# A four-layer graph network on one core: three gather passes go by tile of 128 edges, and edges are ranked four tiles at a time

## The chip, the core and the metric

The kernel runs as one program on one core of a Trainium2 chip. TensorE (PE) multiplies matrices into PSUM, VectorE (DVE), ScalarE (ACT) and GpSimd (POOL) work on SBUF and PSUM, SyncE (SP) here only issues and waits for DMAs. The engines run their own instruction lists and wait for each other by semaphores. The metric is the device time in microseconds (us) of one execution.

## The reference

12,500 nodes with 128 features, 212,500 edges (one loop per node among them) sorted by destination, eight edge types. Each layer takes `h = relu(layernorm(x))`, sums over edges, and adds the result to `x`:

```python
def _rel_graph_conv(x, W, W_loop, b, src, dst, etypes, num_nodes):      # layer 0, twice, relu between
    xw = jnp.einsum('nd,rdh->rnh', x, W)
    agg = jax.ops.segment_sum(xw[etypes, src], dst, num_segments=num_nodes)
    return agg + x @ W_loop + b
# layer 1: edge_index = stack([src, dst]), so rows are summed by SOURCE
h = x @ W.T + b
agg = jax.ops.segment_sum(h[col], row, N) / (cnt + 1e-08)
h = h + agg;  out = batchnorm(h) * gamma + beta
# layer 2: attention with 4 heads over the edges of a source (segment max, exp, sum)
# layer 3: mean of the rows that arrive
sums = jax.ops.segment_sum(x[edge_src], edge_dst, N) / max(counts, 1)
```

## The kernel before

Nodes stand as 98 blocks of 128 in SBUF (`X`, `ACC`, node in its partition). Edges in order of destination form `ET` = 1661 tiles of 128. A **step** is one tile together with one block of nodes: where a tile's destinations lie in two blocks, the tile has two steps. There are at most 1758 steps, padded to `NS` = 1760, in `NG` = 220 groups of `K` = 8; four groups (`RING` = 4) are in flight. Tables made in the first stage say for each step which block it belongs to (`BREGA`) and which edge each partition has (`IDXA` the row of the table, `DLOA` the destination less the block's first node); registers are loaded from such tables by `words_of` (line 436).

A sum over edges, as in `plain_pass` (lines 1031 to 1087), works step by step. ACT copies the indices of eight steps (line 1045), POOL issues eight indirect DMAs that gather 128 rows each (`gather`, line 1025), DVE builds eight one-hot matrices in one instruction (`one_hot`, line 970) and PE multiplies one-hot by rows (line 1085), which sums the rows of a node; DVE adds each product to its block in `ACC`, at an address from a register (line 1074). `groups` and `ringed` write the loops, four groups to an iteration, each with its slots and semaphores.

The order of the stages: `tables_and_first` (rows of the first table TAB for eight relations on PE, and beside them the edge tables on DVE, POOL and PE, put between PE's blocks by hand with `upto`), `ranked_pass`, `dense`, `plain_pass` "g1", `square`, `scatter_pass`, `message_pass`, batch norm, `square`, `largest_pass`, `attention_pass`, a short stage, `plain_pass` "g3".

Layer 1 needs sums by source, so `ranked_pass` (lines 1089 to 1198) also finds each edge's place in the order of sources: `RK` in PSUM holds, for each partition and block of sources, how many edges came before. For each step PE adds the strictly upper triangle times the one-hot of the key (`KO`, line 1192), DVE reads `RK` at the edge's own key (line 1149), then PE adds the rest (line 1197), so PE and DVE take turns for each step. Edges that don't belong to the step's block get a key that matches nothing, and a place beyond the end. `scatter_pass` (lines 1200 to 1279) fetches for each edge the row of its destination by a product with the turned one-hot and scatters it to its place in MSG, one indirect DMA a step (line 1275); DVE prepares the source (line 1233), ACT the places (line 1214). `message_pass` reads MSG in order.

## Time and profile before

| | us |
|---|---|
| median of 3 runs (lowest to highest) | 13794.56 (13775.52 to 13798.18) |
| the profiled execution, its own time | 13784.63 |
| its span, first to last instruction | 13782.6 |
| busy: POOL, PE, DVE, ACT | 9051.3 (66%), 8229.3 (60%), 7417.8 (54%), 1688.7 (12%) |
| mean granted TensorE clock | 0.70 |

Busy shares are averages over stages with different limits: what bounds a stage is read from who waits in it. Instructions that work on registers, branch, issue or wait aren't counted as busy. The time that an indirect DMA shows on POOL is that of making its descriptors, not of moving the rows.

### The profile page before, as it was taken

To read this page: it belongs to the slowest core of one execution; us is meant where nothing else is said; L and a number is where in the kernel's file an instruction comes from. 1 tells how busy PE (TensorE), PEld (TensorE's weight loads), DVE (VectorE), ACT (ScalarE), POOL (GpSimd) and SP (SyncE) were. 2 spreads that over 40 slices of the span, in tenths; PEclk is the share of its full clock that TensorE was granted. 3 is DMA by queue.
4 is the path that set the end of the run, shared out by engine and by line. 5 is a ranking of instruction groups with operands and counts; after the bars stand their busy time and mean duration, and the time that the engine had idled before them with its cause. 6 is when DMAs were issued, how large, how long until landed. Compare 5 with 4: busy or idle time off the path is not lost. (4 is left out here: it accounts for less than half of the span.)

```text
span 13782.6 us, 185595 instructions
## 1 busy us (share of the span) xinstructions
PE 8229.3 (60%) x41562; PEld 5943.6 (43%) x41563; DVE 7417.8 (54%) x19952; ACT 1688.7 (12%) x3723; POOL 9051.3 (66%) x9488
## 2 busy tenths in 40 slices
PE   8555555743333345454546969999998993333333
PEld 4444444433333344444445743333336772333333
DVE  4666666533333343332336977777778884333333
ACT  4000000100000011111110021111113552000000
POOL 0777777367777757777773127777775554777776
PEclk9666666865555565656567978888889996555555
DMA  4222212422212211111114833333333433222222
GB/s 175 64 53 53 53 53 53 147 75 53 53 53 53 53 54 49 50 50 50 50 50 130 205 98 106 106 104 106 104 105 112 127 126 78 54 54 54 54 54 66
DMA packets 715974, 1096.30 MB, mean 80 GB/s; under 512 B 181713, under 2 KB 490913, under 8 KB 715892
## 3 DMA queue, kind: packets, MB, share of 16 engines
q0 software_dynamic: 282496, 584.15, 16.4%
q1 hardware_dynamic: 301480, 449.08, 9.8%
...
## 5 line engine op out<-in xcount | busy, mean ns | idle before, releaser
L1027 POOL DMA_INDIRECT G<-HROW,IDS x3520 | 3334.2, 947 | 1451.8 <-issue 1120.3
L1027 POOL DMA_INDIRECT G<-TAB,IDS x3520 | 3327.1, 945 | 1405.8 <-issue 1072.0
L1085 PE MATMUL PSUM<-G,OH 128*128 128x128 f32 (+1 forms) x7040 | 1645.6, 427 | 2894.5 <-DMA G<-HROW,IDS 1506.5
L1085 PEld LDWEIGHTS PSUM<-G,OH 128*128 128x128 f32 x7040 | 1527.7, 329 | 3012.2 <-issue 2816.9
L1074 DVE TENSOR_TENSOR ACC<-ACC,PSUM 128x128 f32 (+1 forms) x3520 | 1017.1, 289 | 2855.2 <-PE PSUM L1085 2409.6
L1275 POOL DMA_INDIRECT MSG<-G,IDS x1760 | 1734.4, 985 | 649.3 <-issue 584.8
L1589 DVE TENSOR_REDUCE SM<-PSUM 128x8 f32<-128x1024 f32 x880 | 1074.4, 1221 | 390.3 <-PE PSUM L1527 379.1
L1193 PE MATMUL PSUM<-G,OH 128*128 128x128 f32 x3520 | 1197.2, 453 | 0.0
L1262 PE MATMUL PSUM<-ACC,SCR 128*128 x3520 | 812.1, 424 | 628.4 <-ACT SCR L1218 628.0
L971 DVE TENSOR_TENSOR OH<-PSUM,DLOA 128x1024 f32<-128x1024 f32 x880 | 1073.1, 1220 | 94.4 <-DVE POSA L1166 55.4
L1262 PEld LDWEIGHTS PSUM<-ACC,SCR 128*128 128x128 f32 x3520 | 754.8, 326 | 699.6 <-issue 699.6
L1192 PE MATMUL PSUM<-SCR,USTB 128*128 128x98 bf16 x1760 | 473.5, 269 | 910.3 <-DMA G<-TAB,IDS 715.3
L992 PE MATMUL PSUM<-G,OH 128*128 128x129 f32 (+1 forms) x7040 | 881.6, 279 | 29.5 <-DVE OH L971 27.5
L992 PEld LDWEIGHTS PSUM<-G,OH 128*128 128x128 f32 x7040 | 840.3, 191 | 106.3 <-issue 88.2
L1193 PEld LDWEIGHTS PSUM<-G,OH 128*128 128x128 f32 x3520 | 881.5, 307 | 0.0
L1716 POOL TENSOR_TENSOR G<-G 128x1024 f32<-128x1024 f32 x220 | 555.0, 2523 | 418.7 <-ACT G L1742 418.7
L1240 DVE COPY G<-PSUM 128x256 f32<-128x256 f32 x880 | 332.7, 420 | 772.7 <-PE PSUM L1262 772.4
L1527 PE MATMUL PSUM<-SCR,WT 128*128 128x512 bf16 x1760 | 722.4, 410 | 0.0
L1526 PE MATMUL PSUM<-SCR,WT 24*128 24x512 bf16 x1760 | 693.4, 394 | 0.0
L1149 DVE CUSTOM_DVE_ANT_0 HT<-PSUM,SCR 128x98 f32<-128x98 f32 x1760 | 456.3, 259 | 421.6 <-PE PSUM L1192 410.3
L1539 PE MATMUL PSUM<-USTB,LINB 128*128 128x512 bf16 x1760 | 661.2, 544 | 0.0
L999 DVE TENSOR_TENSOR ACC<-ACC,PSUM 128x1188 f32 x440 | 611.0, 1389 | 89.5 <-PE PSUM L992 89.3
...
## 6 DMA issues: line engine op xcount, KB each, us to landing
KEEP<-G SPq DMA_DIRECT2D x220, 528.0 KB, 2.8
G<-KEEP SPq DMA_DIRECT2D x220, 528.0 KB, 3.5
...
G<-TAB,IDS POOLq DMA_INDIRECT x3520, 2.5
G<-HROW,IDS POOLq DMA_INDIRECT x3520, 2.5
...
```

What stands on the lines that cost most here:

```text
L971: return q.tensor_tensor(OH[:, r % 2], bcast(iota.unsqueeze(1), P, K, P), bcast(dlo[:, bass.ds(g * K, K)].unsqueeze(2), P, K, P), op)
L992: return q.matmul(window(n)[:, bass.ds(off, w)], hot, rows, start=False, stop=False, skip_group_check=True)
L1027: q.indirect_dma_start(G[:, r, k, 0:row], None, table, bass.IndirectOffsetOnAxis(ap=IDS[:, r, k:k + 1], axis=0)).then_inc(s_got[r], 16)
L1074: q.tensor_tensor(a, a, sums(r, k), ALU.add).then_inc(s_add, 1)
L1085: m = q.matmul(sums(r, k), OH[:, r % 2, k, :], G[:, r, k, 0:w], start=True, stop=True)
L1193: m = q.matmul(slot(kk)[:, 0:w], OH[:, r % 2, kk, :], G[:, r, kk, 0:w], start=True, stop=True)
L1262: m = q.matmul(slot(h * 4 + k)[:, 0:D], SCR[:, h, k * P:(k + 1) * P], acc_of(regs[h * 4 + k], D), start=True, stop=True)
L1275: q.indirect_dma_start(MSG, bass.IndirectOffsetOnAxis(ap=IDS[:, r, k:k + 1], axis=0), G[:, r, k, :], None, bounds_check=E - 1, oob_is_err= ...
L1526: q.matmul(bank, SEL[:, k, :], ROWS[r % 2], start=True, stop=False)
L1527: m = q.matmul(bank.rearrange("p (h e) -> p h e", h=HEADS), NEGI, bcast(TURN[r % 2][:, k, :].unsqueeze(1), P, HEADS, P), start=False, stop ...
L1539: q.matmul(PS[6], LINB[:], bcast(USTB[:].unsqueeze(1), P, 4, P), start=True, stop=True)
L1589: q.tensor_reduce(reduced(n), PSUM[:, (n % 2) * 1024:(n % 2 + 1) * 1024].rearrange("p (h e) -> p h e", e=P), AX.X, ALU.max).then_inc(s_red, 1)
```

## The change

`ranked_pass`, `plain_pass` "g1" and "g3" gather by tile of 128 edges: `NTG` = 208 groups of eight tiles, each into one of the four slots of the ring. Steps stay for the products: `SLOTS` gives for each step where in `G` its tile lies (an address in a register), and for each group of steps how many tile groups must have landed; SP counts landings into one semaphore (`tile_landings`). `LASTA` gives for each tile group the step group after which its slot may be written again; ACT loads it and waits before it copies the indices. `IDXA` and the places `POSA` are now by tile, `DLOA` by step.

Ranks are made per tile, four at once: PE makes the counts inside four tiles (`within`, products of 392, 294, 196 and 98 columns), DVE copies `RK`, adds, multiplies by the one-hot of the keys and sums (`places`, twice a group), and PE adds the four to `RK` (`counted`). What belongs to the step's block is decided in `scatter_pass`, where DVE fetches place and source of each step by its tile (sixteen one-column instructions) and makes the target from them.

The tables stage makes the tables for both; the rows of the edge table are now read once by step (destinations) and once by tile (source and type), in 27 turns instead of 14, and the second half starts at block 67 instead of 60.

```diff
+NTG = -(-ET // (K * RING)) * RING
...
-BREGA, BREGB, TREGB = (REGS[i * 32:i * 32 + 1, 0:SW] for i in range(3))
+SLOTS = REGS[0:1, 0:NG * (K + 1)].rearrange("o (g k) -> o g k", k=K + 1)
+LASTA = REGS[0:1, NG * (K + 1):NG * (K + 1) + NTG]
+BREGB, TREGA, TREGB, BREGA = (REGS[at:at + 1, i * NS:(i + 1) * NS] for at in (32, 64) for i in range(2))
...
-for col in range(SC):
-    if col >= 2:
-        q.wait_ge(s_tix, col)
-    q.indirect_dma_start(EGI[col % 2], None, ET1,
-                         bass.IndirectOffsetOnAxis(ap=TIX[:, col:col + 1], axis=0)).then_inc(s_eg, 16)
-    q.wait_ge(s_eg, 16 * (col + 1))
+for i in range(SC + CHUNKS):
+    if i >= 2:
+        q.wait_ge(s_tix, i)
+    if i < SC:
+        q.indirect_dma_start(EGI[i % 2], None, ET1,
+                             bass.IndirectOffsetOnAxis(ap=TIX[:, i:i + 1], axis=0)).then_inc(s_eg[i % 2], 16)
+    else:
+        t, n = tiles_of(i - SC)
+        q.dma_start(EGI[i % 2][0:n, P:3 * P], ET1[t:t + n, P:3 * P]).then_inc(s_eg[i % 2], 16)
...
+tile = TMPW[0:1, 0:NS].bitcast(I32)
+c.step(q.tensor_copy(tile, SELX[0:1, 0:NS]))
+tile8 = tile.rearrange("o (g k) -> o g k", k=K)
+c.step(q.tensor_scalar(SLOTS[:, :, K], tile8[:, :, K - 1], 3, None, ALU.arith_shift_right))
+c.inc(q.tensor_scalar(SLOTS[:, :, K], SLOTS[:, :, K], 1.0, None, ALU.add))
+c.step(q.tensor_scalar(tile, tile, K * RING - 1, None, ALU.bitwise_and))
+c.step(q.tensor_scalar(SLOTS[:, :, 0:K], tile8, float(RW), None, ALU.mult))
...
+c.step(q.tensor_scalar(TMPW[:, 0:NS], SELX[:, 0:NS], UPTO[:, i:i + 1], 0.0, ALU.is_le, ALU.add,
+                       accum_out=STEPS[:, i:i + 1]))
...
+c.step(q.tensor_scalar(LASTA[:, RING:NTG], last[:, 0:NTG - RING], 1.0, None, ALU.add))
...
-for s, cnt, first in ((0, CNTA, 17), (1, CNTB, 60)):
+for s, cnt, first in ((0, CNTA, 17), (1, CNTB, 67)):
...
+upto(first + 28 + i * 3 // 4)
+n = P if i < SC else tiles_of(i - SC)[1]
+q.wait_ge(s_tix, i + 2)
+q.transpose(side(1 + i)[:, 0:n], EGF[0:n, 0:P], IDENT[0:n, 0:n]).then_inc(s_pe, 1)
...
+def tile_ids(q, s_mm, per, s_ids):
+    def body(j, r, t):
+        if not is_first(j):
+            [n] = words_of(q, LASTA, t, 1, NG)
+            q.wait_ge(s_mm, n * per)
+        q.copy(IDS[:, r, :], IDXA[:, bass.ds(t * K, K)]).then_inc(s_ids, 1)
+    tile_rings(q, body)
+def tile_gathers(q, s_ids, table, row, s_got):
+    def body(j, r, t):
+        wait(q, s_ids, t + 1)
+        q.nop(nofuse=True)
+        gather(q, r, table, row, s_got)
+    tile_rings(q, body)
+def tile_landings(q, s_got, s_land):
+    def body(j, r, t):
+        q.wait_ge(s_got[r], 16 * K * (j + 1))
+        q.sem_inc(s_land, 1)
+    tile_rings(q, body)
+def landed_rows(q, g, w, s_land):
+    words9 = words_of(q, REGS[0:1, :], g * (K + 1), K + 1, [(K * RING - 1) * RW] * K + [NTG])
+    q.wait_ge(s_land, words9[K])
+    return [GW[:, bass.ds(at, w)] for at in words9[0:K]]
...
-q.wait_ge(s_got[r], 16 * K * (j + 1))
+rows = landed_rows(q, g, w, s_land)
 q.wait_ge(s_oh, g + 1)
 wait(q, s_add, (g - 1) * K)
 for k in range(K):
-    m = q.matmul(sums(r, k), OH[:, r % 2, k, :], G[:, r, k, 0:w], start=True, stop=True)
+    m = q.matmul(sums(r, k), OH[:, r % 2, k, :], rows[k], start=True, stop=True)
...
-q.wait_ge(s_rk, 2 * (g * K + kk) + 2)
-q.tensor_tensor_reduce(out=HT[:, 0, 0:NB], in0=RK, in1=KO[:, r % 2, kk, :], scale=1.0, scalar=0.0,
-                       op0=ALU.mult, op1=ALU.add, accum_out=SM[:, 5, kk:kk + 1]).then_inc(s_pos, 1)
...
+def keys(r, t):
+    if not is_tile(t):
+        return
+    q.tensor_scalar(KEYI, IDXA[:, bass.ds(t * K, K)], 10, None, ALU.arith_shift_right).then_inc(s_kb, 1)
+    q.wait_ge(s_kb, 2 * t + 1)
+    q.tensor_copy(KEYF, KEYI).then_inc(s_kb, 1)
+    q.wait_ge(s_kb, 2 * t + 2)
+    wait(q, s_rk, 2 * (t - 1) + 1)
+    q.tensor_tensor(KO[:, r % 2], bcast(IOTP[:, 0:NB].unsqueeze(1), P, K, NB),
+                    bcast(KEYF.unsqueeze(2), P, K, NB), ALU.is_equal).then_inc(s_key, 1)
+def places(r, t, h):
+    if not is_tile(t):
+        return
+    at, own_keys = PLACE[h], KO[:, r % 2, h * HALF:(h + 1) * HALF, :]
+    q.wait_ge(s_rk, 2 * t + h + 1)
+    q.tensor_copy(SOFAR[h], RK).then_inc(s_far, 1)
+    q.wait_ge(s_w, 2 * t + h + 1)
+    q.wait_ge(s_far, 2 * t + h + 1)
+    q.tensor_tensor(at, WITHIN[h].rearrange("p (k b) -> p k b", k=HALF), bcast(SOFAR[h].unsqueeze(1), P, HALF, NB),
+                    ALU.add).then_inc(s_t, 1)
+    q.wait_ge(s_t, 2 * t + h + 1)
+    q.tensor_tensor(at, at, own_keys, ALU.mult).then_inc(s_pos, 1)
+    q.wait_ge(s_pos, 4 * t + 2 * h + 1)
+    q.tensor_reduce(POSA[:, bass.ds(t * K + h * HALF, HALF)], at, AX.X, ALU.add).then_inc(s_pos, 1)
+def body(j, r, g):
+    hot(r + 1, g + 1)
+    keys(r + 1, g + 1)
+    regs = blocks(q, BREGA, g)
+    for h in range(2):
+        places(r, g, h)
+        add_half(q, s_mm, s_add, regs[h * HALF:(h + 1) * HALF], g, h, w)
...
+def within(r, t, h):
+    if not is_tile(t):
+        return
+    if h == 0:
+        q.wait_ge(s_key, t + 1)
+    wait(q, s_t, 2 * (t - 1) + h + 1)
+    q.matmul(WITHIN[h], USTB[:], KO[:, r % 2, h * HALF:(h + 1) * HALF, :].rearrange("p k b -> p (k b)"), start=True, stop=False,
+             skip_group_check=True)
+    for k in range(HALF - 1):
+        n = HALF - 1 - k
+        m = q.matmul(WITHIN[h][:, (k + 1) * NB:].rearrange("p (k b) -> p k b", k=n), ONESB[:],
+                     bcast(KO[:, r % 2, h * HALF + k, :].unsqueeze(1), P, n, NB), start=False, stop=k == HALF - 2,
+                     skip_group_check=True)
+    m.then_inc(s_w, 1)
+def counted(r, t, h):
+    if not is_tile(t):
+        return
+    q.wait_ge(s_far, 2 * t + h + 1)
+    for k in range(HALF):
+        m = q.matmul(RK, ONESB[:], KO[:, r % 2, h * HALF + k, :], start=False, stop=False, skip_group_check=True)
+    m.then_inc(s_rk, 1)
 def body(j, r, g):
-    q.wait_ge(s_got[r], 16 * K * (j + 1))
+    rows = landed_rows(q, g, w, s_land)
     q.wait_ge(s_oh, g + 1)
-    q.wait_ge(s_key, g + 1)
     for h in range(2):
-        wait(q, s_add, (g - 1) * K + (h + 1) * K // 2)
-        for k in range(4):
-            kk = h * 4 + k
-            i = g * K + kk
-            q.matmul(RK, USTB[:], KO[:, r % 2, kk, :], start=False, stop=False, skip_group_check=True).then_inc(s_rk, 1)
-            m = q.matmul(slot(kk)[:, 0:w], OH[:, r % 2, kk, :], G[:, r, kk, 0:w], start=True, stop=True)
-            if k == 3:
-                m.then_inc(s_mm, 1)
-            q.wait_ge(s_pos, i + 1)
-            q.matmul(RK, LINB[:], KO[:, r % 2, kk, :], start=False, stop=False, skip_group_check=True).then_inc(s_rk, 1)
-groups(q, body)
+        wait(q, s_add, (g - 1) * K + (h + 1) * HALF)
+        for k in range(h * HALF, (h + 1) * HALF):
+            m = q.matmul(slot(k)[:, 0:w], OH[:, r % 2, k, :], rows[k], start=True, stop=True)
+        m.then_inc(s_mm, 1)
+        within(r, g, h)
+    for h in range(2):
+        counted(r, g, h)
+passes(q, body)
...
+q.wait_ge(s_x, MOVES * g + 2 * K + 3)
 wait(q, s_sc[r], 16 * K * j)
-q.copy(IDS[:, r, :], POSA[:, bass.ds(g * K, K)]).then_inc(s_ids, 1)
+q.copy(IDS[:, r, :], SM[:, r, 3 * K:4 * K]).then_inc(s_ids, 1)
...
+tile = words_of(q, REGS[32:33, :], g * K + NS, K, ET - 1)
+place, srci, out_, to = (SM[:, r, i * K:(i + 1) * K] for i in range(4))
+srci = srci.bitcast(I32)
+dlo = DLOA[:, bass.ds(g * K, K)]
+for k in range(K):
+    q.tensor_copy(place[:, k:k + 1], POSA[:, bass.ds(tile[k], 1)]).then_inc(s_x, 1)
+    q.tensor_scalar(srci[:, k:k + 1], IDXA[:, bass.ds(tile[k], 1)], 3, None, ALU.arith_shift_right).then_inc(s_x, 1)
+q.tensor_scalar(out_, dlo, 0.0, None, ALU.is_lt).then_inc(s_x, 1)
+q.wait_ge(s_x, MOVES * g + 2 * K + 1)
+q.scalar_tensor_tensor(out_, dlo, float(P - 1), out_, ALU.is_gt, ALU.add).then_inc(s_x, 1)
+q.wait_ge(s_x, MOVES * g + 2 * K + 2)
+q.scalar_tensor_tensor(to, out_, FAR, place, ALU.mult, ALU.add).then_inc(s_x, 1)```

The order on DVE in one round of the ranked pass, from the one-hot of the keys (`SCR<-PSUM,SM`) on; first before:

```order
L1134 TENSOR_TENSOR SCR<-PSUM,SM 128x784 [waits work5]
L441 ISA
L441 TENSOR_LOAD REGS
L443 ISA
L1147 ISA [waits work3,work2]
L1147 TENSOR_TENSOR ACC<-ACC,PSUM 128x128
```

Then each addition to `ACC` stands between two reads of the rank. Now:

```order
L1240 TENSOR_TENSOR SCR<-PSUM,SM 128x784 [waits work13,work7]
L447 ISA
L447 TENSOR_LOAD REGS
L449 ISA
L1249 COPY HT<-PSUM 128x98 [waits work13]
L1252 TENSOR_TENSOR WT<-PSUM,HT 128x392 [waits work10,work9]
L1255 TENSOR_TENSOR WT<-WT,SCR 128x392 [waits work11]
L1256 ISA
L1257 REGISTER_ALU [waits work12]
L1257 TENSOR_REDUCE POSA<-WT 128x4
L1081 ISA [waits work3,work2]
L1081 TENSOR_TENSOR ACC<-ACC,PSUM 128x128
```

Four instructions in a chain now stand ahead of four additions, twice a round, where a read of the rank stood ahead of each addition.

The order on DVE in one round of the scatter pass, from the one-hot to the copies of the rows; `scsc0` is the semaphore of the scatters that used the slot before. Before:

```order
L971 TENSOR_TENSOR OH<-PSUM,DLOA 128x1024
L422 REGISTER_ALU
L1233 REGISTER_ALU [waits scsc0]
L1233 TENSOR_SCALAR SM<-IDXA 128x8
L1234 REGISTER_ALU
L1234 COPY G<-DSTA 128x8
L1235 ISA
L1236 CAST G<-SM 128x8 [waits work2]
L1238 ISA
L1240 COPY G<-PSUM 128x2x128 [waits work5]
```

Now:

```order
L1029 TENSOR_TENSOR OH<-PSUM,DLOA 128x1024
L428 REGISTER_ALU
L447 ISA [waits scsc0]
L447 TENSOR_LOAD REGS
L449 ISA
L1356 REGISTER_ALU
L1356 COPY SM<-POSA 128x1
L1357 REGISTER_ALU
L1357 TENSOR_SCALAR SM<-IDXA 128x1
L1356 ISA
L1356 COPY SM<-POSA 128x1
L1357 REGISTER_ALU
```

A register load and sixteen such instructions (two for each of eight steps) stand between the wait for the scatters and what ACT copies to the indices.

## Rows read from the trace of the kernel before

**Rows 1.** windows: engine busy us (x instructions), PEclk, DMA share, GB/s; ranked, first plain pass

```profile
367.00:2583.00 2216.00, 1281.70 (x7042) 1024.86 (x7042) 1545.82 (x7048) 42.97 (x220) 1666.69 (x1760) 0.64 0.20 52
2808.00:5012.00 2204.00, 821.24 (x3520) 762.32 (x3520) 763.58 (x2003) 43.00 (x218) 1652.16 (x1752) 0.58 0.20 52
```

**Rows 2.** waits: engine, tile and line, who ended it: us, times, longest

```profile
PE PSUM L1085 <- DMA G<-HROW,IDS: 1506.5, 220, 138.8
```

**Rows 3.** timeline, ranked pass, POOL: start us, us, instruction [idle before <- releaser]

```profile
367.88 2.17 POOL L1027 DMA_INDIRECT G<-TAB,IDS  x1 [107.05 <-ACT IDS L1102]
...
382.71 0.94 POOL L1027 DMA_INDIRECT G<-TAB,IDS  x1 [0.30 <-issue]
...
2569.64 0.94 POOL L1027 DMA_INDIRECT G<-TAB,IDS  x1 [0.30 <-issue]
```

**Rows 4.** timeline of DVE, one round of the ranked pass

```profile
1500.28 1.22 DVE L971 TENSOR_TENSOR OH<-PSUM,DLOA 128x1024 f32<-128x1024 f32 x1 [0.64 <-DVE POSA L1166]
1501.42 0.16 DVE L1127 TENSOR_SCALAR SM<-IDXA 128x8 int32 x1
...
1502.13 0.17 DVE L1133 SCALAR_TENSOR_TENSOR SM<-SM 128x8 f32<-128x8 f32 x1
1502.33 0.97 DVE L1134 TENSOR_TENSOR SCR<-PSUM,SM 128x784 bf16<-128x784 f32 x1
1503.51 0.29 DVE L1147 TENSOR_TENSOR ACC<-ACC,PSUM 128x128 f32 x1 [0.21 <-issue]
...
1509.96 1.22 DVE L971 TENSOR_TENSOR OH<-PSUM,DLOA 128x1024 f32<-128x1024 f32 x1 [0.16 <-DVE POSA L1166]
```

**Rows 5.** source line 441 (words_of): ns min/median/max, first and last start us

```profile
L441 DVEq TENSOR_LOAD <-REGS x881: 355/598/1387, 383.5 to 13736.5; - x177
```

**Rows 6.** timeline of DVE, one round of the first plain pass

```profile
3501.34 3.29 DVE L1074 TENSOR_TENSOR ACC<-ACC,PSUM 128x128 f32 x8 [5.25 <-PE PSUM L1085]
3504.55 1.22 DVE L971 TENSOR_TENSOR OH<-PSUM,DLOA 128x1024 f32<-128x1024 f32 x1
```

**Rows 7.** timeline of DVE, start of the ranked pass

```profile
367.20 14.38 DVE L1119 TENSOR_TENSOR ACC<-ACC,BIAS 128x1792 f32<-128x1792 f32 x7
```

**Rows 8.** source line 1597, DVE, pass for the largest scores

```profile
L1597 DVE TENSOR_TENSOR MJ<-MJ,SM x1760: 146/161/228, 8199.7 to 10458.1; 128x4 f32 x196
```

**Rows 9.** source line 1027: the gathers from HROW

```profile
L1027 POOL DMA_INDIRECT G<-HROW,IDS x3520: 938/944/14022, 8163.4 to 13736.5; - x196
```

**Rows 10.** timeline of POOL and DVE, start of the pass for the largest scores

```profile
8163.43 14.02 POOL L1027 DMA_INDIRECT G<-HROW,IDS  x1 [185.66 <-ACT IDS L1469]
...
8165.67 10.84 DVE L1550 MEMSET ACC<- 128x12936 f32 x1 [2.65 <-issue]
```

**Rows 11.** timeline of DVE and ACT, scatter pass, running free and later

```profile
5147.27 1.22 DVE L971 TENSOR_TENSOR OH<-PSUM,DLOA 128x1024 f32<-128x1024 f32 x1
...
5149.39 1.10 ACT L1218 COPY SCR<-PSUM 128x512 f32<-128x512 f32 x2 [5.58 <-PE PSUM L1256]
...
5154.22 1.22 DVE L971 TENSOR_TENSOR OH<-PSUM,DLOA 128x1024 f32<-128x1024 f32 x1
...
6009.56 0.17 DVE L1233 TENSOR_SCALAR SM<-IDXA 128x8 int32 x1 [3.39 <-DMA MSG<-G,IDS]
...
6009.67 0.18 DVE L1234 COPY G<-DSTA 128x8 f32 x1
```

**Rows 12.** source line 1275, the scatters

```profile
L1275 POOL DMA_INDIRECT MSG<-G,IDS x1760: 982/982/2085, 5107.3 to 7376.5; - x196
```

**Rows 13.** timeline of POOL, DVE and PE, tables stage

```profile
209.21 1.12 POOL L798 DMA_INDIRECT SI<-ET,MJ  x1 [82.21 <-DVEq L886]
...
212.41 0.36 DVE L890 CAST G<-SI 128x384 f32<-128x384 int32 x1 [3.55 <-DMA SI<-ET,MJ]
...
219.99 1.88 PE L916 MATMUL PSUM<-WT,HT 128*128 128x512 f32 x4
...
222.04 1.45 PE L916 MATMUL PSUM<-WT,HT 128*128 128x512 f32 x3
```

More of the change, by code:

```diff
@@ L945, in _ @@
                             q.matmul(side(n)[:, 0:w], BW[:, 0, :], SELX[0:NB, k:k + w], start=True, stop=True).then_inc(s_pe, 1)
-                        if s:
-                            for n, (k, w) in enumerate(WIDE):
-                                upto(first + 16 + n)
-                                v += 1
-                                q.wait_ge(s_v, v)
-                                q.matmul(side(n)[:, 0:w], BW[:, 1, :], SELX[0:NB, k:k + w], start=True, stop=True).then_inc(s_pe, 1)
+                        if not s:
+                            upto(first + 14)
+                            v += 1
+                            q.wait_ge(s_v, v)
+                            for col in range(SC):
+                                last = q.matmul(side(0)[:, col:col + 1], SELX[0:NB, col * P:(col + 1) * P], RH[:, 1:2], start=True, stop=True)
+                            last.then_inc(s_pe, 1)
@@ L952, in _ @@
+                        for n, (k, w) in enumerate(WIDE):
+                            upto(first + 16 + n)
+                            v += 1
+                            q.wait_ge(s_v, v)
+                            q.matmul(side(n)[:, 0:w], BW[:, 1, :], SELX[0:NB, k:k + w], start=True, stop=True).then_inc(s_pe, 1)
+                        if s:
                             continue
-                        upto(first + 14)
+                        upto(first + 26)
                         v += 1
@@ L1028, in gather, with tile_rings, ring @@
                                      bass.IndirectOffsetOnAxis(ap=IDS[:, r, k:k + 1], axis=0)).then_inc(s_got[r], 16)
+        def tile_rings(q, body):
+            def ring(j):
+                for r in range(RING):
+                    body(j, r, j * RING + r)
+            loop(q, NTG // RING, ring)
+        def tile_ids(q, s_mm, per, s_ids):
[20 more added lines that the diff above has]
+            return [GW[:, bass.ds(at, w)] for at in words9[0:K]]
         def plain_pass(tag, table, row, w):
             fresh()
-            s_ids, s_oh, s_mm, s_add, s_io = (own(tag + n) for n in ("ids", "oh", "mm", "add", "io"))
+            s_ids, s_oh, s_mm, s_add, s_io, s_land = (own(tag + n) for n in ("ids", "oh", "mm", "add", "io", "land"))
             s_got = [sem(tag + f"got{r}") for r in range(RING)]
@@ L1097, in ranked_pass, with passes, ring, is_tile @@
+            def passes(q, body):
+                def ring(j):
+                    for r in range(RING):
+                        body(j, r, j * RING + r)
+                ring(0)
+                with q.Fori(1, ranked - 1) as j:
+                    ring(j)
+                for j in range(ranked - 1, NG // RING):
+                    ring(j)
+            def is_tile(t):
+                return not isinstance(t, int) or t < NTG
             with nc.Block() as block:
+                @block.sync
+                def _(q):
+                    tile_landings(q, s_got, s_land)
@@ L1111, in _ @@
-                    groups(q, body)
+                    tile_gathers(q, s_ids, table, row, s_got)
                 @block.vector
                 def _(q):
-                    c = Chain(q, s_cs)
                     q.tensor_copy(IOTP, IOTA[:]).then_inc(s_io, 1)
                     q.wait_ge(s_io, 1)
-                    for n in range(NCH):
-                        c.step(q.tensor_tensor(ACC[:, chunk(n), 0:D], ACC[:, chunk(n), 0:D], bcast(BIAS[:, 0:D].unsqueeze(1), P, CH, D), ALU.add))
-                    ahead = c.n
@@ L1169, in ring @@
-                    def ring(j):
-                        for r in range(RING):
-                            body(j, r, j * RING + r)
-                    ring(0)
-                    per = c.n - ahead
-                    with q.Fori(1, NG // RING) as j:
-                        c.at, c.n = per * j + ahead, 0
-                        ring(j)
-                    add_half(q, s_mm, s_add, words_of(q, BREGA, NS - K // 2, K // 2, NB - 1), NG - 1, 1, w)
+                    def keys(r, t):
[8 more added lines that the diff above has]
+                                        bcast(KEYF.unsqueeze(2), P, K, NB), ALU.is_equal).then_inc(s_key, 1)
@@ new lines, in body @@
+                    def body(j, r, g):
[5 more added lines that the diff above has]
+                            add_half(q, s_mm, s_add, regs[h * HALF:(h + 1) * HALF], g, h, w)
+                    for n in range(NCH):
+                        q.tensor_tensor(ACC[:, chunk(n), 0:D], ACC[:, chunk(n), 0:D], bcast(BIAS[:, 0:D].unsqueeze(1), P, CH, D),
+                                        ALU.add).then_inc(s_bias, 1)
@@ L1179, in _ @@
+                    hot(0, 0)
+                    keys(0, 0)
+                    q.wait_ge(s_bias, NCH)
+                    passes(q, body)
                 @block.tensor
@@ L1198, in _ @@
-                    groups(q, body)
+                            wait(q, s_add, (g - 1) * K + (h + 1) * HALF)
[5 more added lines that the diff above has]
+                            counted(r, g, h)
+                    passes(q, body)
@@ L1204, in scatter_pass @@
             BET = HT[:, 1, :]
+            MOVES = 2 * K + 5
             with nc.Block() as block:
```

178 lines of the change are left out of this document (82 added, 96 removed).

## The prediction, made before the changed kernel ran

> **What bounds the kernel now.** I read the windows by stage first, then the waits, then single rounds in the timeline. In the stretch of the ranked pass and in that of the first plain pass [rows 1] no engine is full: in the plain pass POOL is busy 1652 us of 2204, PE 821, DVE 764, and the DMA share is 0.20. The reader is to see that two passes with very different work on DVE (1546 us against 764 us) take the same time. What they share is 1760 gathers on POOL. The waits say who is late: PE waits for the gathered rows, 220 times, once a group [rows 2]. The timeline of POOL gives the price: the gathers of the ranked pass number 8 to 1760 start from 382.71 to 2569.64 [rows 3], 1752 gaps, so 1.2483 us each, of which 0.94 us is busy and 0.30 us lies between two. The plain pass has the same busy time a gather (1652.16 us over 1752, [rows 1]), so a gather has a price on POOL and nothing that DVE or PE does makes it cheaper. A group of eight is 9.99 us.
>
> **Gathers by tile.** There are 1661 tiles of 128 edges; the steps are padded to 1760, the tile groups to 208, so 1664 gathers. Each of the three passes loses 96 gathers: 96 x 1.2483 = 119.8 us where POOL stays the bound, 359.5 us in all. The fourth gather of this kind (the one for the largest scores) and the scatter keep 1760.
>
> **The two plain passes.** DVE per group: one 1.22 us one-hot and eight additions in 3.21 us [rows 6], 4.4 us, now against a step group each 1664 x 1.2483 / 220 = 9.44 us. PE has 821 us of 2204 [rows 1] and gains a load of nine registers, about 0.6 us for eight on DVE [rows 5], while it waits for rows. Steps and tiles no longer match, so a group of steps can need two groups of tiles, and a slot comes free after the step group that uses its last tile; that is one group (10 us) later at most, with four slots in the ring, so POOL doesn't wait. SP only counts landings. I take the full 119.8 us twice: -239.7. If that cover failed, POOL would show waits for ACT's copy of the indices, one period of 9.99 us per stall.
>
> **The ranked pass.** Here DVE is nearly as full as POOL: before, one round runs from 1500.28 to 1509.96 [rows 4]. Its new round, from rows:
> - one-hot, to the next issue: 1501.42 - 1500.28 = 1.14 us;
> - two small key instructions, each waiting for the last: 2 x 0.20 (1502.33 - 1502.13) = 0.40;
> - keys one-hot, and behind it the load of eight registers (598 ns, [rows 5]): 1503.51 - 1502.33 = 1.18;
> - each half: a copy of 98 columns, an addition and a product of 392, a sum of 392. The length goes by columns: 1.22 us for 1024 [rows 4], 0.29 for 128, so 1.04 ns a column and 0.15 us fixed; seven with two inputs in SBUF, 14.38 us for 1792 columns each [rows 7], lie on the same line (2.05 us against 2.02), and I put the sum there too. So 0.26, and 0.56 three times; 0.03 us more where one waits for the other (0.20 less 0.17), 0.08 less at the end (1.22 less 1.14): 0.29 + 0.59 + 0.59 + 0.48 = 1.95;
> - four additions to the sums at 3.21 / 8 = 0.40 [rows 6]: 1.60.
>
> Round: 1.14 + 0.40 + 1.18 + 2 x (1.95 + 1.60) = 9.82 us. A step group should come every 9.44 us, so DVE, not POOL, sets the pace while there are tiles to rank, 208 rounds: 2043 us. The step groups run ahead of nothing then; at the end of round 208 some 197 tile groups are used, POOL has issued three or four more (the ring), and the last 8 follow at its own price, 8 x 9.99 = 80 us. Together 2123 us, against 1760 x 1.2483 = 2197 before: -74 us, not -120. PE isn't late: its new products on bf16 keys are issued between DVE's copy and DVE's next half, 3.5 us later; and the handover for each tile between PE and DVE of the old scheme (eight a group) is gone.
>
> **What DVE takes from POOL.** At the start of the pass, DVE adds the bias with both inputs in SBUF for those 14.38 us; from 367.88 to 382.71 POOL started 7 gathers, 2.12 us apart, so 7 x 0.87 = 6.1 us were lost, 0.42 us for each us of such work. The new product (line 1255 of the changed kernel) is of that kind, 2 x 0.56 = 1.12 us a tile group. At the same rate that is 0.47 us a group, 98 us in all, and POOL's own floor rises from 2077 to 2175. At the other end, the 1760 updates of MJ from MJ and SM, both in SBUF but 4 columns wide [rows 8], leave the gathers of that pass at a median of 944 ns [rows 9]. 392 columns lie between; I take a third, 33 us, 2110 us, which hides behind DVE's 2123. Both ends, 2077 and 2175, stay for the range. The Trainium skill (SBUF — State Buffer, "Who interferes with whom") says that a tensor_tensor with two SBUF inputs takes only the shared read interface and that descriptors need the write interface, marked there as inferred; by it the product would delay nothing. It also says that the shared pair is a lock and the loser blocks fully. This trace agrees with the second (a gather of 14.02 us beside a memset of 10.84 us, [rows 10]) and not with the first, and the measurement decides.
>
> **The scatter pass.** It stays at 1760 scatters, 5107.3 to 7376.5 [rows 12], 1.290 us each, 10.3 us a group. But DVE's round grows: a load of registers, sixteen one-column instructions that fetch place and source by tile, and three that make the target, all ahead of ACT's copy of the indices, and ACT's copies of the turned one-hot are queued behind that one, then PE's products, DVE's copies, and the next one-hot. This loop is closed. While scatters had not yet landed it ran free at 5154.22 - 5147.27 = 6.95 us, with ACT's copy 2.12 us after the one-hot [rows 11]. Now ACT starts after 1.14 (the register load lies under the one-hot) + 16 p + 0.07 + 3 x 0.20 + 0.30. For p, two instructions that each need a register computed start 0.11 us apart [rows 11]; with the 0.02 us longer kind in half of them, 0.12. That is 4.0 us, loop 6.95 + 1.9 = 8.9 us, under 10.3. POOL stays the bound and only the first group starts later: +3 us. Cover: 1.4 us a group. It is gone at p = 0.21.
>
> **Tables stage.** PE's products for the tables set the pace there, a block each 222.04 - 219.99 = 2.05 us. Four more products and two small ones, fewer transposes: +2 us. The loop over columns now turns 27 times each 0.75 block, two turns 3.08 us, and a gathered column needs from its issue to its use 212.41 - 209.21 = 3.2 us [rows 13], plus the handover: 14 turns stall 0.2 us or more: +4. Bounds 0 and +20 (2.5 us a turn). I take +6.
>
> **Sum.** -239.7 - 74 + 3 + 6 = -305. The profiled execution took 13784.63 us (its span is 13782.6), so 13480; the median of the runs shown is 10 us above it, and I put the forecast between, 13485.
>
> **Rivals.**
> A. DVE's round in the ranked pass is longer than counted (handovers through semaphores at 0.1 us more for six of them, 10.4 us): 208 x 10.4 + 80 = 2243, +46 in place of -74. For it: 0.58 us more eats it all, and the sum has 26 instructions in a chain. Against: the rows used already hold their waits. Time 13605; half way 13545.
> B. DVE keeps up and the product costs POOL nothing: the pass falls to 2077, all three gain 119.8: 13440. For it: the small products that delay no gather [rows 8, 9] and the idle time inside the old round (0.64 and 0.21 us, [rows 4]). The Trainium skill (SBUF — State Buffer, "Who interferes with whom") would have it so for the product.
> C. Slower than before, by one mechanism: the sixteen fetches in the scatter pass. If each took 0.40 us, as DVE's chained additions with a register do, ACT would start at 8.5 us, the loop be 13.3 us, 220 x 3.0 = +660: 14145. It costs from p = 0.21 and turns the whole change slower from a loop of 10.3 + 305 / 220 = 11.7 us, p = 0.30. Against it: they wait for nothing, and the two small instructions in [rows 11] start 0.11 us apart.
> D. The ring holds POOL back, since steps and tiles are out of phase: each pass keeps its 10 us per step group, nothing gained but the overheads: 13790. Against it: four slots, 30 us of lead.
>
> **How the numbers follow.** Forecast 0.60 (own range 13455 to 13515); A 0.17; B 0.15; C 0.05, of which 0.03 is slower than before; D 0.03. The range 13430 to 13570 takes B and the nearer half of A. Within 0.2% (27 us, about what a measurement can tell) is D, 0.02; slower 0.03; faster 0.95.
>
> **What would show it.** Right: 1664 gathers a pass, still 1.25 us apart in the plain passes, each some 120 us shorter; in the ranked pass POOL waiting for ACT's index copy through the middle (DVE without gaps, a round near 9.8 us) and no more in the last 80 us; some gathers there longer than 0.95 us; scatters still 1.29 us apart, with ACT's index copy about 4 us behind the one-hot or the landing. Wrong: POOL waiting for ACT in a plain pass (D), scatters waiting for DVE's copies to G (C), or a DVE round in the ranked pass over 10.4 us (A) or with gaps and POOL full (B).

## The result and the profile after

| us | before | changed |
|---|---|---|
| median (lowest to highest) | 13796.2 (13775.52 to 13798.18, 4 runs) | 13545.15 (13543.68 to 13551.77, 4 runs) |
| span of the profiled run | 13782.6 | 13541.9 |
| ranked pass, first to last gather | 2201.8 | 2188.8 |
| plain pass g1 | 2195.5 | 2075.8 |
| scatter, first to last | 2269.2 | 2269.5 |
| largest scores | 2272.2 | 2261.9 |
| plain pass g3 | 2195.6 | 2075.8 |

The ratio is 0.9822, 95% interval 0.9805 to 0.9839: 1.8% shorter, by 251 us of medians, 240.7 us of spans. The forecast was 13485, the range 13430 to 13570, so the time is inside the range, but 60 us above the forecast and outside the narrower range of 13455 to 13515 that the forecast was given. The two plain passes gave what was forecast, the ranked pass 13 us where 74 were forecast.

One word on the engines as they were introduced: GpSimd (POOL) touches only SBUF and HBM in this kernel; no row of its trace reads or writes PSUM.

Windows by stage (length; PE, weight loads, DVE, ACT, POOL busy us; clock, DMA share, GB/s; as [rows 1]), ranked pass and first plain pass:

```profile
376.00:2580.00 2204.00, 1240.88 (x6848) 1045.90 (x6848) 1803.30 (x4275) 40.27 (x204) 1590.34 (x1664) 0.67 0.17 50
2805.00:4885.00 2080.00, 801.73 (x3520) 745.91 (x3520) 755.57 (x1975) 40.24 (x204) 1561.63 (x1656) 0.60 0.18 52
```

In the plain pass 1656 gathers fill 2080 us as 1752 filled 2204. In the ranked pass POOL has 1664 gathers too, but DVE has risen from 1546 to 1803 busy us: 82% of the stretch. Most of the rest are short steps from one instruction to the next in a chain, too short to be shown as idle time. Timeline of POOL, first and last gather of both passes, to be read against [rows 3]:

```profile
376.17 2.23 POOL L1085 DMA_INDIRECT G<-TAB,IDS  x1 [84.97 <-ACT IDS L1102]
...
2564.95 0.94 POOL L1085 DMA_INDIRECT G<-TAB,IDS  x1 [0.30 <-issue]
...
2794.22 0.94 POOL L1085 DMA_INDIRECT G<-TAB,IDS  x1 [228.32 <-ACT IDS L1102]
...
4870.05 0.94 POOL L1085 DMA_INDIRECT G<-TAB,IDS  x1 [0.30 <-issue]
```

2075.83 over 1663 gaps is 1.248 us a gather, as before. Waits inside the ranked pass (us in total, times, longest), which answer to [rows 2]:

```profile
ACT IDS L1102 <- PE PSUM L1310: 2125.9, 204, 22.1
POOL G L1085 <- ACT IDS L1102: 179.8, 42, 85.0
PE PSUM L1301 <- DVE HT L1249: 410.3, 225, 3.3
PE PSUM L1310 <- DVE ACC L1081: 327.0, 136, 3.2
PE PSUM L1310 <- SPq L1117: 175.4, 56, 17.0
DVE ACC L1081 <- PE PSUM L1310: 46.3, 9, 7.6
```

This is a chain read backwards: POOL waits for ACT's indices (the first 85 us are the start, so 95 us inside the pass), ACT for PE's products, PE mostly for DVE (its copy of `RK`, then its additions), and DVE for nobody: its 46 us of waiting for PE all lie behind the last ranked tile, and from 389 to 2479 us, while tiles are ranked, all its idle times together are 32 us of 2090. In these rounds DVE sets the pace. Two rounds of DVE in that pass, against [rows 4]:

```profile
485.66 1.22 DVE L1029 TENSOR_TENSOR OH<-PSUM,DLOA 128x1024 f32<-128x1024 f32 x1
486.79 0.16 DVE L1235 TENSOR_SCALAR SM<-IDXA 128x8 int32 x1
486.99 0.17 DVE L1237 CAST SM<-SM 128x8 f32<-128x8 int32 x1
487.20 0.97 DVE L1240 TENSOR_TENSOR SCR<-PSUM,SM 128x784 bf16<-128x784 f32 x1
488.18 0.26 DVE L1249 COPY HT<-PSUM 128x98 f32<-128x98 f32 x1
488.54 0.57 DVE L1252 TENSOR_TENSOR WT<-PSUM,HT 128x392 f32<-128x392 f32 x1
489.14 0.57 DVE L1255 TENSOR_TENSOR WT<-WT,SCR 128x392 f32<-128x392 f32 x1
489.83 0.56 DVE L1257 TENSOR_REDUCE POSA<-WT 128x392 f32 x1
490.31 1.57 DVE L1081 TENSOR_TENSOR ACC<-ACC,PSUM 128x128 f32 x4
491.79 0.25 DVE L1249 COPY HT<-PSUM 128x98 f32<-128x98 f32 x1
...
495.42 1.22 DVE L1029 TENSOR_TENSOR OH<-PSUM,DLOA 128x1024 f32<-128x1024 f32 x1
...
1498.99 1.22 DVE L1029 TENSOR_TENSOR OH<-PSUM,DLOA 128x1024 f32<-128x1024 f32 x1
1500.12 0.41 DVE L1235 TENSOR_SCALAR SM<-IDXA 128x8 int32 x1
1500.57 0.17 DVE L1237 CAST SM<-SM 128x8 f32<-128x8 int32 x1
...
1509.00 1.22 DVE L1029 TENSOR_TENSOR OH<-PSUM,DLOA 128x1024 f32<-128x1024 f32 x1
```

No row has idle time before it. The first round is 9.76 us, the second 10.01; the difference is in the small key instruction, 0.41 us in place of 0.16. Over the 208 rounds (391.5 to 2479.5) the mean is 10.04 us.

Scatter pass, DVE and ACT, against [rows 11], and the line of the scatters, against [rows 12]:

```profile
6005.32 1.22 DVE L1029 TENSOR_TENSOR OH<-PSUM,DLOA 128x1024 f32<-128x1024 f32 x1
...
6007.68 0.15 DVE L1356 COPY SM<-POSA 128x1 f32 x1 [1.15 <-issue]
6007.79 0.15 DVE L1357 TENSOR_SCALAR SM<-IDXA 128x1 int32 x1
...
6009.54 0.16 DVE L1358 TENSOR_SCALAR SM<-DLOA 128x8 f32 x1
...
6010.13 0.20 ACT L1333 CAST IDS<-SM 128x8 int32<-128x8 f32 x1 [9.06 <-DVE SM L1362]
```

```profile
L1403 POOL DMA_INDIRECT MSG<-G,IDS x1760: 982/982/2302, 4990.8 to 7260.3; - x196
```

The sixteen fetches take 6009.54 - 6007.68 = 1.86 us, 0.116 each, and the scatters still come 1.290 us apart.

### The profile page after: what moved, and what is told of

Read it like the earlier page. It is cut to its first block and busy times, and to the rows that moved or that the text cites. A ratio compares the mean times of both kernels' runs of the same rounds, so it can differ in the third digit from the quotient of the medians.

```text
span 13541.9 us, 197710 instructions
## 1 busy us (share of the span) xinstructions
PE 8145.6 (60%) x41367; PEld 5933.2 (44%) x41368; DVE 8125.3 (60%) x21148; ACT 1681.5 (12%) x3687; POOL 8802.5 (65%) x9213
## 5 line engine op out<-in xcount | busy, mean ns | idle before, releaser
L1085 POOL DMA_INDIRECT G<-HROW,IDS x3424 | 3243.8, 947 | 1411.6 <-issue 1087.0
L1085 POOL DMA_INDIRECT G<-TAB,IDS x3328 | 3160.3, 950 | 1419.5 <-issue 1011.3
L1177 PE MATMUL PSUM<-G,OH 128*128 x7040 | 1605.2, 420 | 2700.4 <-SPq L1117 2621.9
L1177 PEld LDWEIGHTS PSUM<-G,OH 128*128 128x128 f32 x7040 | 1492.9, 323 | 2812.6 <-issue 2812.6
L1166 DVE TENSOR_TENSOR ACC<-ACC,PSUM 128x128 f32 (+1 forms) x3520 | 1017.2, 289 | 2624.8 <-PE PSUM L1177 2182.6
L1403 POOL DMA_INDIRECT MSG<-G,IDS x1760 | 1734.7, 986 | 655.6 <-issue 610.8
L1310 PE MATMUL PSUM<-G,OH 128*128 x3520 | 859.0, 422 | 549.5 <-DVE ACC L1081 327.0
L1029 DVE TENSOR_TENSOR OH<-PSUM,DLOA 128x1024 f32<-128x1024 f32 x880 | 1071.9, 1218 | 52.3 <-issue 50.3
L1310 PEld LDWEIGHTS PSUM<-G,OH 128*128 128x128 f32 x3520 | 759.5, 318 | 590.3 <-issue 587.5
L1102 ACT COPY IDS<-IDXA 128x8 int32 (+1 forms) x624 | 122.2, 197 | 6163.4 <-PE PSUM L1177 4026.1
L1050 PEld LDWEIGHTS PSUM<-G,OH 128*128 128x128 f32 x7040 | 839.6, 191 | 99.7 <-issue 81.2
L1081 DVE TENSOR_TENSOR ACC<-ACC,PSUM 128x128 f32 x1760 | 501.0, 285 | 239.3 <-PE PSUM L1310 46.3
```

What stands on the lines that cost most here:

```text
L1029: return q.tensor_tensor(OH[:, r % 2], bcast(iota.unsqueeze(1), P, K, P), bcast(dlo[:, bass.ds(g * K, K)].unsqueeze(2), P, K, P), op)
L1050: return q.matmul(window(n)[:, bass.ds(off, w)], hot, rows, start=False, stop=False, skip_group_check=True)
L1085: q.indirect_dma_start(G[:, r, k, 0:row], None, table, bass.IndirectOffsetOnAxis(ap=IDS[:, r, k:k + 1], axis=0)).then_inc(s_got[r], 16)
L1166: q.tensor_tensor(a, a, sums(r, k), ALU.add).then_inc(s_add, 1)
L1177: m = q.matmul(sums(r, k), OH[:, r % 2, k, :], rows[k], start=True, stop=True)
L1310: m = q.matmul(slot(k)[:, 0:w], OH[:, r % 2, k, :], rows[k], start=True, stop=True)
```

## The experiments

Theory 1: since ranks are made four at once, DVE's round of 10.04 us sets the ranked pass, where POOL alone would take 9.44. Theory 2: POOL sets it, slowed by DVE's product with two SBUF inputs (line 1255). Theory 3: the ring holds POOL, steps and tiles being out of phase.

The three timed sets ran on chips on which every kernel is slower in the passes with POOL's indirect DMAs: the kernel before takes 16301, 16415 and 16310 us there. So whole times are compared inside one set alone, and the changed kernel itself was in set 2 only. The kernel before, run once more on yet another chip, ran there as in the first profiles. Below, an undisturbed chip is one like that, and a disturbed chip one like those of the sets.

| set | kernel | median us | ratio to before, interval | ranked pass, first to last gather |
|---|---|---|---|---|
| 1 | additions 32 wide | 15904.61 | 0.9754 (0.9738 to 0.9771) | 2672.9 |
| 1 | place in PSUM | 15931.6 | 0.9771 (0.9755 to 0.9788) | 2711.7 |
| 1 | four counts | 15906.51 | 0.9750 (0.9733 to 0.9767) | 2663.4 |
| 1 | rank by one | 16202.48 | 0.9936 (0.9919 to 0.9952) | 2965.0 |
| 2 | the changed kernel | 16090.93 | 0.9809 (0.9792 to 0.9825) | 2687.4 |
| 2 | four counts | 16072.65 | 0.9797 (0.9780 to 0.9814) | 2657.2 |
| 2 | rank by one | 16379.57 | 0.9983 (0.9973 to 0.9992) | 2980.1 |
| 2 | keys by ring | 16077.26 | 0.9801 (0.9785 to 0.9817) | 2677.4 |
| 3 | rank by one | 16217.28 | 0.9949 (0.9932 to 0.9965) | 2952.7 |
| 3 | four counts | 15918.79 | 0.9753 (0.9735 to 0.9772) | 2662.3 |
| 3 | place in PSUM | 15934.92 | 0.9770 (0.9754 to 0.9786) | 2686.3 |

**What the chips of the sets do.** First the changed kernel itself, and the kernel before.

> The changed kernel as it is, beside the experiments of this set. In the set before it, every engine waited some us in every fourth group in all passes, also where POOL alone had set the pace (plain passes 2427 us in place of 2076, the kernel before 16301 us in place of 13796), and the changed kernel was not among them. All theories: 13545 us where the chip runs as it did for the profile of the changed kernel; where those waits are there too, about 15945 us, a little over the second experiment's 15932.

> The kernel before itself, for its trace on a chip as these sets have it: in them the kernel before takes 16301 to 16415 us, not 13796, and the changed kernel 16091, not 13545. If the added time is waits of the engines for their own instructions, as the changed kernel's trace of these sets has it (PE in the plain pass: 750 us 'issue' where there was next to none), then this trace shows them too, its plain passes take about 2540 us in place of 2196 (those of the changed kernel 2441 in place of 2076), and the rest of the gain, 324 us less twice 100, is in the ranked pass. If the chip runs as in the first profiles: 13796.

The kernel before took 13788.86 us in its one run (13777.53 for the run beside it), its passes of gathers 2202.5, 2196.3, 2272.2 and 2196.5 us: each repeats within 1 us, so the 13 us of the ranked pass are more than its spread. The changed kernel took 16090.93 us, 0.9809 of before, so the ratio of the change hardly differs. Its plain pass takes 2440.5 us in place of 2075.8. Its timeline there, PE, ACT and DVE, one group:

```profile
5025.54 3.49 PEld L1177 LDWEIGHTS PSUM<-G,OH 128*128 128x128 f32 x16 [6.56 <-issue]
5025.54 3.78 PE L1177 MATMUL PSUM<-G,OH 128*128 x16 [6.27 <-issue]
5037.71 0.20 ACT L1102 COPY IDS<-IDXA 128x8 int32 x1 [27.14 <-remote]
5037.72 0.29 DVE L1166 TENSOR_TENSOR ACC<-ACC,PSUM 128x128 f32 x1 [22.75 <-remote]
```

ACT and DVE both wait for PE's products alone, and both start together, 8 us after PE's last one. From the start of a group's last product to that group's first addition it is 0.57 us in the median of the changed kernel's first trace; here the median is 12.4 us, a tenth under 5.1 and a tenth over 19.3. SyncE still sees a group's rows 2.5 us after the start of its last gather, and PE starts 0.23 us after DVE's one-hot is done. So the word from PE to DVE and ACT arrives late.

It isn't all. DVE and PE also wait for nothing that the profile shows, as my expectation had it. Waits of the changed kernel here, 3300 to 5650 us (us in total, times, longest):

```profile
PE PSUM L1177 <- issue: 749.5, 109, 16.5
DVE ACC L1166 <- issue: 221.8, 91, 11.4
```

The first trace has neither line in its plain pass. DVE's register instructions are slow in the same stretches: 681 of them took over 0.5 us in the pass, 470 us together, against 218 (the register loads) and 130 us in the first trace. Which of the two comes first, and why, stays open. The stages without indirect DMAs are nearly as long as before: 227.8 us from the last gather of the ranked pass to the first of the plain pass (229.3), 791.9 (791.4) in front of the pass for the largest scores, 1115.4 (1101.6) behind it.

**Narrow additions** (leaves out columns 32 to 127 of the ranked pass's sum).

```diff
-add_half(q, s_mm, s_add, regs[h * HALF:(h + 1) * HALF], g, h, w)
+add_half(q, s_mm, s_add, regs[h * HALF:(h + 1) * HALF], g, h, 32)
```

> In the ranked pass the eight additions of a round are 32 columns wide instead of 128; the other 96 columns of that sum are left out. Theory 1 (DVE's own round of 10.04 us sets the ranked pass): each addition is 96 columns x 1.04 ns = 0.10 us shorter, a round 0.80 us, so about 9.24 us, under POOL's 9.44 us a step group; POOL becomes the bound again, the first to last gather fall from 2188.8 us to about 2100, the whole to about 13460. Theory 2 (the product with both inputs in SBUF slows POOL, and POOL sets the pass): nothing on POOL's side changes, same as the changed kernel, 13545. Theory 3 (the ring of four slots holds POOL, steps and tiles being out of phase): 13545 too.

The whole time can't be compared with the changed kernel's, which was in another set. The round can: where DVE finds PE's word there, it goes from one-hot to one-hot in

```profile
1211.19 1.22 DVE L1029 TENSOR_TENSOR OH<-PSUM,DLOA 128x1024 f32<-128x1024 f32 x1
...
1220.22 1.22 DVE L1029 TENSOR_TENSOR OH<-PSUM,DLOA 128x1024 f32<-128x1024 f32 x1
```

9.03 us, 0.73 less than the changed kernel's undisturbed 9.76 (forecast 0.80). So a DVE round under POOL's 9.44 us is reached by taking work from DVE; that the pass would then shorten, by some 85 us as expected, isn't shown.

**Place in PSUM.**

```diff
-PLACE = [WT[:, h * HALF * NB:(h + 1) * HALF * NB].rearrange("p (k b) -> p k b", k=HALF) for h in range(2)]
+PLACE = [a.rearrange("p (k b) -> p k b", k=HALF) for a in WITHIN]
...
-wait(q, s_t, 2 * (t - 1) + h + 1)
+wait(q, s_pos, 4 * (t - 1) + 2 * h + 2)
```

> The sum of counts and so-far counts is written back into PSUM, so that the product that follows has one input in PSUM and only the one-hot of the keys in SBUF; the result is the same. Theory 2 (the product with two SBUF inputs costs POOL): the 68 gathers of the ranked pass that last over 0.98 us go, and the pass falls towards 2077 us, the whole by up to 100 us, to 13445. Theory 1 (DVE's round sets it): the long gathers go too (21 us of POOL time in all), but POOL waits that much longer for ACT, and the pass stays at 2189 within 15 us: 13545, or some us more if operands in PSUM cost DVE more. Theory 3: 13545.

> The product of the ranks reads PSUM and one SBUF operand in place of two in SBUF, on a chip without the waits for instructions. In the first set the gathers longer than normal were 7 with it (98 in the kernel with the narrow additions, which keeps the product). Theory 2 (POOL, slowed by the product, sets the ranked pass): pass 2077 to 2110 us, whole 13450 to 13470. Theory 1 (DVE's round sets it): 7 long gathers, POOL waits 15 us more for ACT, pass 2189 within 15 us, whole 13545, or up to 30 us more if reading and writing PSUM costs DVE more.

Windows of the ranked pass, gathers alone (us, POOL busy, PEclk, DMA share, GB/s), the changed kernel in set 2:

```profile
372.00:3075.00 2703.00, 1601.38 (x1664) 0.65 0.16 40
```

and this kernel in set 3:

```profile
379.00:3080.00 2701.00, 1574.93 (x1664) 0.64 0.16 40
```

26.5 us of POOL's time go, and of 99 gathers over 980 ns 7 are left (those beside the bias). The two ran in different sets, but four counts, which has no such product either and ran in set 2, shows the same: 1575.2 us, and 7. The pass does not shorten: 2687.4 us in set 2 against 2711.7 in set 1 and 2686.3 in set 3, and in those two sets the plain pass is 13 us shorter than in set 2. DVE's undisturbed round is 9.80 us, no shorter. So the product does lengthen gathers, and taking that away gains nothing here. Against theory 2 also speaks the first trace, in which POOL itself waits 95 us for ACT inside the pass: it isn't the bound there.

**Four counts.** The counts of four tiles stand in one PSUM bank; PE adds more, DVE neither copies nor adds.

```diff
-q.tensor_copy(SOFAR[h], RK).then_inc(s_far, 1)
-q.tensor_tensor(at, WITHIN[h].rearrange("p (k b) -> p k b", k=HALF), bcast(SOFAR[h].unsqueeze(1), P, HALF, NB), ALU.add).then_inc(s_t, 1)
-q.tensor_tensor(at, at, own_keys, ALU.mult).then_inc(s_pos, 1)
+q.tensor_tensor(at, RK, own_keys, ALU.mult).then_inc(s_pos, 1)
...
+q.matmul(RK, LINB[:], keys_of(r, h), start=False, stop=False, skip_group_check=True)
+for k in range(1, HALF):
+    m = add_to(0, k, k, r, h)
```

> The running count is kept four times in one PSUM bank, one for each tile of a half; PE adds what each tile needs, and DVE multiplies and sums straight from there: per half a copy of 98 columns (0.38 us) and an addition of 392 (0.60 us) are gone, 1.96 us a round, while PE gets 980 more columns a half (about 0.9 us each at the clock of that pass). Theory 1: DVE's own round is 8.1 us, or about 8.7 with one wait for PE, under 9.44 us; POOL is the bound, the ranked pass is 2077 us of gathers and 7 to 15 at its start, 2085 to 2095 in place of 2189, the whole about 13445. If PE (7.9 us of work a round, and in turn with DVE) becomes the bound at 9.8 us a round: 2135, 13490. Theory 2 (POOL slowed by the product): the product has no second SBUF input either, so it gives the same gain; only the second experiment tells these two apart. Theory 3 (ring): 13545.

> The same kernel as the experiment with four running counts, to be read against the changed kernel in one set. Theory 1 (DVE's round of 10.04 us sets the ranked pass): round 8.1 to 8.7 us, POOL the bound, ranked pass 2085 to 2095 us, whole 90 to 100 us under the changed kernel (13445). Theory 3 (the ring holds POOL): no change. Where the waits of the first set are there, the gain is about 40 us (2663 against 2712 us in the ranked pass there).

> Four running counts in one PSUM bank, on a chip without the waits for instructions. Theory 1: DVE's round falls from 10.04 to 8.1 to 8.7 us, under POOL's 9.44; ranked pass 2085 to 2095 us, whole 13440 to 13455. If PE and DVE in turn need 9.8 us a round: 13490. Theory 3 (the ring holds POOL): 13545.

```profile
2259.74 1.23 DVE L1029 TENSOR_TENSOR OH<-PSUM,DLOA 128x1024 f32<-128x1024 f32 x1 [0.33 <-issue]
...
2262.38 0.57 DVE L1248 TENSOR_TENSOR WT<-PSUM,SCR 128x392 f32<-128x392 f32 x1
2263.08 0.56 DVE L1250 TENSOR_REDUCE POSA<-WT 128x392 f32 x1
...
2267.72 1.22 DVE L1029 TENSOR_TENSOR OH<-PSUM,DLOA 128x1024 f32<-128x1024 f32 x1
```

The shortest rounds are 7.98 us (8.1 expected; the rows shown are one of them), and the ranked pass is the shortest in all three sets, by 30 us beside the changed kernel. In the whole that is 18 us, less than the intervals tell apart. Since 7.98 is under POOL's 9.44 us, POOL would be the bound on an undisturbed chip: an estimate, from 1664 gathers at 1.248 us and 7 to 15 us at the start, is 2085 to 2095 us for the pass and some 95 us less in all. It is the version to try next, not one shown to win.

**Keys by ring.** The shift and the cast of the keys are made once for four groups, 32 columns wide.

> The two small key instructions of the ranked pass (shift, cast) are made once for four groups of tiles, 32 columns wide, in place of once a group; the result is the same. Theory 1: DVE's round loses 0.75 x (0.289 + 0.235) = 0.39 us and is 9.65 us; the pass is 13 + 208 x 9.65 + 94 = 2114 us in place of 2189, the whole 13470 (75 us less). If POOL's delays by DVE's product come up behind it: 2130, 13485. Theory 2 (POOL slowed by the product sets the pass) and 3 (ring): 13545.

In three groups of four the round has no small key instructions and is 9.32 us where nothing is late:

```profile
1353.54 1.23 DVE L1029 TENSOR_TENSOR OH<-PSUM,DLOA 128x1024 f32<-128x1024 f32 x1
1354.68 0.96 DVE L1241 TENSOR_TENSOR SCR<-PSUM,SM 128x784 bf16<-128x784 f32 x1
...
1362.87 1.23 DVE L1029 TENSOR_TENSOR OH<-PSUM,DLOA 128x1024 f32<-128x1024 f32 x1
```

Beside the changed kernel in set 2 the pass shortened by 10 us, the whole by 14, within the intervals. The gain in the round is there (0.44 us in those three, 0.33 on average, expected 0.39), its worth in the pass is not shown.

**Rank by one.** Gathers by tile, but ranks as before, one tile at a time.

```diff
-q.tensor_reduce(POSA[:, bass.ds(t * K + h * HALF, HALF)], at, AX.X, ALU.add).then_inc(s_pos, 1)
+q.wait_ge(s_rk, 2 * (g * K + kk) + 2)
+q.tensor_tensor_reduce(out=HT[:, 0, 0:NB], in0=RK, in1=KO[:, r % 2, kk, :], scale=1.0, scalar=0.0,
+                       op0=ALU.mult, op1=ALU.add, accum_out=SM[:, 5, kk:kk + 1]).then_inc(s_pos, 1)
```

> Half of the change is undone: rows are still gathered by tile, but ranks are made one tile at a time, as in the kernel before (PE adds, DVE reads with a multiply and sum, PE adds), for the 208 groups of tiles. Theory 1 (DVE's round sets the ranked pass since ranks are made four at once): the old round was 9.68 us, of which about 0.3 us was waiting for rows, and three of its five small key instructions (0.5 us) are gone: 8.9 us, under 9.44; POOL is the bound, the pass falls from 2189 to about 2085 us, the whole to 13440. So this half of the change cost about 100 us where it stands. If the turns between PE and DVE set a floor of 9.7 us instead: 208 x 9.7 and the tail, 2125, 13480. If ranks four at once save DVE time, as the change has it: slower than 13545. Theory 3 (ring): 13545.

> The same kernel as the experiment with ranks made one tile at a time, against the changed kernel in one set. In the first set its ranked pass took 2965 us against 2663 to 2712 of the others, so ranks one at a time suffer most from those waits. Theory 1, where they are absent: DVE's round is 8.9 us, POOL the bound, pass 2085 us, 100 us under the changed kernel, 13440. If the turns between PE and DVE are a bound of their own (9.7 us and more a round): 13480 or more; if ranks four at once save time, over 13545.

> Ranks one tile at a time with gathers by tile, on a chip without the waits for instructions. Theory 1 (DVE's round of 10.04 us, made by ranking four at once, sets the ranked pass): DVE's round is 8.9 us, POOL the bound at 9.44, the ranked pass 2085 us in place of 2189, whole 13440. Rival (the turns between PE and DVE are a bound of their own): 9.7 us a round, 2125 us, 13480. Rival (ranks four at once do save time here, as they did by 290 us where instructions came late): over 13545.

Slower than the changed kernel by 289 us in its set (0.9983 against 0.9809, intervals far apart), all in the ranked pass: 2980.1 against 2687.4. My expectation of a gain failed there. One round of DVE:

```profile
1504.13 1.22 DVE L1029 TENSOR_TENSOR OH<-PSUM,DLOA 128x1024 f32<-128x1024 f32 x1
...
1508.68 0.26 DVE L1253 CUSTOM_DVE_ANT_0 HT<-PSUM,SCR 128x98 f32<-128x98 f32 x1 [0.21 <-PE PSUM L1292]
...
1512.25 0.26 DVE L1253 CUSTOM_DVE_ANT_0 HT<-PSUM,SCR 128x98 f32<-128x98 f32 x1 [1.05 <-remote]
...
1515.09 0.26 DVE L1253 CUSTOM_DVE_ANT_0 HT<-PSUM,SCR 128x98 f32<-128x98 f32 x1 [2.37 <-remote]
...
1517.83 1.22 DVE L1029 TENSOR_TENSOR OH<-PSUM,DLOA 128x1024 f32<-128x1024 f32 x1
```

13.7 us a round. DVE waits for PE's counts eight times for eight tiles, and some of them come late; with four at once it waits twice a half, four times a round. That this is why the new ranking wins on such a chip fits the rows, but nothing else was changed to test it. On an undisturbed chip it is open: the shortest rounds here are 8.5 to 9.0 us, under 9.44, so this half of the change may have cost time where it was first timed; no run there tells.

Theory 3 was tested by no experiment; the plain passes, with the same ring, gained all of their 119.8 us, which speaks against it.

So theory 1 rests on the changed kernel's first trace, in which DVE has next to no idle time while tiles are ranked and POOL, PE and ACT wait. The experiments show that DVE's round falls below POOL's price when work is taken from it; none ran on an undisturbed chip, so none shows the pass follow. A second set of fetches in the scatter pass, and 1760 gathers in the new scheme, were not tried.

## Why the prediction was right, and where it was off

**Gathers by tile, the plain passes: right.** -119.7 and -119.8 us against -119.8 each. POOL is the bound, its gather costs 1.248 us, and DVE's and PE's work lies beside it; POOL does not wait there.

**The ranked pass: mechanism right, size wrong.** DVE sets it, as the step said; -13 us in place of -74. (The pass before took 2201.8 us, 5 more than the 2197 of the sum, for its first gathers stand beside the bias.) The step was "Round: 9.82 us" times 208, and 80 for the last groups, 2123. Measured from the first gather (376.17): 15.3 us until the first round, 208 rounds in 2088 us where 2043 were counted (+45), and 85.5 us from there to the last gather (+5): 2189. Three terms:
- The undisturbed round is 9.76 us, but by errors that cancel: the register load runs under the keys' one-hot (0.98 us, not 1.18), four additions take 1.48 (not 1.60), the product 0.69 and the copy 0.36 (not 0.59 and 0.29). What the sum lacked are the disturbances, and they make most of the 0.28 us from 9.76 to 10.04: the small key instruction has a mean of 0.29 us to the next start, not 0.20, the second one 0.23, and the loop's turn, once in four rounds, costs 0.4 us, 0.10 a round. The sum had nothing for them.
- The start: while the bias is added, DVE ranks nothing. Then come the first one-hots, 2.4 us. As the bound had moved to DVE, those 15 us had to be counted on DVE.
- The tail: at the end of round 208 POOL had issued 1595 gathers, so 69 were left, not 64.

**What DVE takes from POOL: right in kind, too dear.** The price of the product was put at 33 us between 0 and 98. POOL's busy time was 1590.34 us in the first trace; without the product it is 1575 (place in PSUM and four counts): 15 us, and 26 in set 2. It hides behind DVE, as said. The 98 came from the bias addition at the same price for each us of DVE's work, and that rate does not hold for this product. The prediction set the Trainium skill (SBUF — State Buffer, "Who interferes with whom"), by which such a product delays nothing, against the trace; by that rule these 15 us would be 0, and the measurement decides against it, by little.

**Scatter: right.** p was put at 0.12 and is 0.116; ACT's copy comes 4.8 us after the one-hot (4.0), since the fetches begin 2.4 us after it, not 1.1. The cover of 1.4 us held: pitch unchanged, the first scatter 6.2 us later after the plain pass (forecast 3). Rival C fell.

**Tables: right.** +8.3 us until the first gather, forecast +6.

**The sum.** Not forecast at all: the pass for the largest scores is 10.3 us shorter (the kernel before repeats its 2272.2 us, so the change did it; how stays open), and the stretches between the passes and behind the last are 7 us longer. That these two nearly cancel is luck. -239.5 - 13.0 + 8.3 + 6.5 - 10.3 + 7.2 = -240.8. Rival A came nearest: the time lies at its half way, 13545, with a round of 10.04, not 10.4; part of the miss is the start and the tail, which A did not have. Two figures in A are off: 0.36 us more a round already eats the 74 us (0.58 leads to +46), and the rows summed are 21 instructions, not 26. B and D fell, B because DVE did not keep up.
